# A graph network's dense stage: who adds x to the product, TensorE or VectorE, and over how many PSUM banks

## The reference, cut to what matters

```
def _L0_gnn_ref(Z, U, Dmat, head_w, edge_index):
    ...
    alpha = exp_l / (seg_sum[:, dst] + 1e-16)
    weighted = alpha[..., None] * zs
    agg = jax.vmap(lambda w_: jax.ops.segment_sum(w_, dst, num_segments=N))(weighted)
    w = jax.nn.softmax(head_w)
    ssa = jnp.einsum('k,knr,kdr->nd', w, agg, U)
    Z_half = (1.0 - C) * Z + C * ssa
    DZ = Z_half @ Dmat.T
    residual = Z_half - DZ @ Dmat
    grad_step = Z_half + ETA * (residual @ Dmat)
    return jax.nn.relu(grad_step - ETA * LAM)
...
x = _layernorm(x + _L0_gnn_ref(x, L0_gnn_U, L0_gnn_Dmat, L0_gnn_head_w, edge_index), axis=-1)
x = _layernorm(x + _L1_gnn_ref(x, edge_index, L1_gnn_weight, L1_gnn_attn_l, L1_gnn_attn_r), axis=-1)
```

## Time and profile before

| | us |
|---|---|
| median of 3 runs | 3771.14 |
| lowest and highest run | 3765.44, 3793.86 |
| profiled execution, its own time | 3755.32 |
| its span | 3753.5 |
| dense stage, first to last product | 98.70 |
| last stage behind it | 334.40 |

### The profile page before, as it was taken

The page is one execution under the profiler, slowest core; times in us unless marked ns, Lnnn a source line. Parts: engine busy times, 40 slices in busy tenths (PEclk is TensorE's granted clock), DMA queues, the critical chain, the costliest instruction groups (busy, mean ns, idle before and its releaser), DMA issues. The chain is left out here.

```text
span 3753.5 us, 61674 instructions
## 1 busy us (share of the span) xinstructions
PE 1961.4 (52%) x15249; PEld 1492.6 (40%) x15250; DVE 1919.1 (51%) x5861; ACT 1169.7 (31%) x3041; POOL 1721.7 (46%) x1833
## 2 busy tenths in 40 slices
PE   7344545454555445445445455354444554594776
PEld 7233434333343333333334334243333333453665
DVE  6344545445555445545455455455445544682566
ACT  2012222323323232323223232223232323353557
POOL 3544454444444444444444444544544444224662
PEclk8555555555555555555555555555555555597877
DMA  6211211121221212211112112121211121293343
GB/s 208 52 37 38 48 42 43 39 46 41 48 47 43 44 40 45 47 40 44 42 38 46 42 41 47 41 48 41 47 38 44 40 47 38 65 314 115 120 139 98
DMA packets 406592, 232.96 MB, mean 62 GB/s; under 512 B 284096, under 2 KB 371434, under 8 KB 406506
## 3 DMA queue, kind: packets, MB, share of 16 engines
q1 hardware_dynamic: 346666, 154.11, 15.0%
q0 software_dynamic: 59840, 77.87, 9.7%
HBM read 134.80 MB, written 42.55 MB: 47 GB/s over the span
## 5 line engine op out<-in xcount | busy, mean ns | idle before, releaser
L549 POOL DMA_INDIRECT arena<-z_table,sslot x1563 | 1487.8, 952 | 1702.9 <-SPq L400 1191.5
L1303 PE MATMUL bank<-arena 128*128 x4992 | 609.5, 228 | 564.2 <-issue 474.7
L1538 ACT ACTIVATE arena<-bank 128x272 f32<-128x272 f32 x416 | 268.4, 662 | 1614.6 <-remote 983.0
L1303 PEld LDWEIGHTS bank<-arena 128*128 128x128 bf16 x4992 | 469.3, 107 | 708.9 <-issue 616.4
L850 DVE TENSOR_TENSOR xin<-arena,bank 128x512 f32<-128x512 f32 x208 | 142.9, 687 | 1034.3 <-remote 697.3
L1515 ACT ACTIVATE acc<-xTb 128x68 f32 x1600 | 386.6, 312 | 350.1 <-issue 339.6
L1320 PE MATMUL bank<-xto,arena 128*128 128x68 bf16 x3328 | 330.7, 246 | 218.9 <-issue 218.8
L1320 PE MATMUL bank<-arena 128*128 128x68 bf16 x1664 | 300.3, 244 | 211.1 <-issue 135.0
L1320 PEld LDWEIGHTS bank<-xto,arena 128*128 128x128 bf16 x3328 | 284.7, 132 | 242.1 <-issue 241.7
L1291 PE MATMUL bank<-ident_b,arena 128*128 128x128 bf16 x1664 | 211.0, 306 | 317.9 <-remote 132.1
L841 DVE TENSOR_SCALAR arena<-iota_b,didx 128x128 bf16<-128x128 bf16 x1664 | 302.0, 264 | 40.8 <-issue 34.2
(11 more groups left out here) (250 smaller groups left out, 2493.2 us busy)
## 6 DMA issues: line engine op xcount, KB each, us to landing
arena<-arena SPq DMA_DIRECT2D x1660, 32.0 KB
arena<-z_table,sslot POOLq DMA_INDIRECT x1563
dspace<-in_xT SPq DMA_DIRECT2D x49, 256.0 KB
xmz_table<-agn SPq DMA_DIRECT2D x49, 256.0 KB
x_table<-arena SPq DMA_DIRECT2D x14, 896.0 KB, 4.9
arena<-in_x SPq DMA_DIRECT2D x13, 896.0 KB, 11.0
out<-arena SPq DMA_DIRECT2D x12, 896.0 KB
xin<-in_xT SPq DMA_DIRECT2D x8, 896.0 KB
```

The source lines that it names most:

```text
L549: pool.indirect_dma_start(ring[:, e % RING, :], None, z_table, bass.IndirectOffsetOnAxis(ap=sslot[:, e:e + 1], axis=0)).then_inc(tiles_in[ ...
L1303: last = T.matmul(zd_ps[g % 2][:, u * KR:(u + 1) * KR], onehotT[:, g * G + u, :], z3[:, bass.ds(tiles[u], 1), s, :].rearrange("p a c -> p ...
L1538: A.activation(sums[:, :, 1 + q * Q:1 + (q + 1) * Q].rearrange("p c j -> p j c"), sum_ps[q % 2][:, 0:Q * AW].rearrange("p (j c) -> p j c", ...
```

## The change

`ADDED_BY_PE` becomes (0, 1, 2, 4, 5, 6): TensorE does the second product in six tiles of a group and VectorE its addition in tile 3 alone. The dense stage rotates over six banks (`YD` = 6, banks 2 to 7), so TensorE waits for tile n - 6. The last stage keeps `YB` = 4. One line more at the top shifts all lines behind it by one.

```diff
--- before.py
+++ after.py
@@ -75,8 +75,9 @@
 HALVES = ((0, 4), (4, T7))
 YT = 2
 NY = NT // YT
-ADDED_BY_PE = (0, 2, 4, 6)
+ADDED_BY_PE = (0, 1, 2, 4, 5, 6)
 YB = 4
+YD = 6
 ROOM = NT * D + 64
 GB = 4
 WARM = 64
@@ -1063,7 +1064,7 @@
 
             def add_rows(n):
                 g, t = n // T7, n % T7
-                summed = psum[2 + n % YB][:, 0:D] if t in ADDED_BY_PE else xmz_buf[g % XB][:, t, :]
+                summed = psum[2 + n % YD][:, 0:D] if t in ADDED_BY_PE else xmz_buf[g % XB][:, t, :]
                 return V.scalar_tensor_tensor(row(n), summed, 0.0, row(n), ALU.max, ALU.add)
 
             added = 0
@@ -1076,7 +1077,7 @@
                     dve.wait_ge(y_ps, k + 1)
                     if t not in ADDED_BY_PE:
                         b = xmz_buf[g % XB][:, t, :]
-                        V.tensor_tensor(b, psum[2 + k % YB][:, 0:D], b, ALU.add).then_inc(y_summed, 1)
+                        V.tensor_tensor(b, psum[2 + k % YD][:, 0:D], b, ALU.add).then_inc(y_summed, 1)
                 if 1 <= k <= NT:
                     n = k - 1
                     if n % T7 not in ADDED_BY_PE:
@@ -1415,21 +1416,21 @@
             keep_busy(WARM // 4)
             for n in range(NT):
                 g, t = n // T7, n % T7
-                if n >= YB:
-
-                    if (n - YB) % T7 in ADDED_BY_PE:
-                        pe.wait_ge(y_added, n - YB + 1)
+                if n >= YD:
+
+                    if (n - YD) % T7 in ADDED_BY_PE:
+                        pe.wait_ge(y_added, n - YD + 1)
                     else:
-                        pe.wait_ge(y_summed, summed_by_dve(n - YB))
+                        pe.wait_ge(y_summed, summed_by_dve(n - YD))
                 if t % 4 == 0:
 
                     pe.wait_ge(aT_ready, 2 * g + t // 4 + 1)
                 by_pe = t in ADDED_BY_PE
-                last = T.matmul(psum[2 + n % YB][:, 0:D], aT[g % 2][:, t * P:(t + 1) * P], w3[:, :], start=True, stop=not by_pe)
+                last = T.matmul(psum[2 + n % YD][:, 0:D], aT[g % 2][:, t * P:(t + 1) * P], w3[:, :], start=True, stop=not by_pe)
                 if by_pe:
                     if t == ADDED_BY_PE[0]:
                         pe.wait_ge(xmz_in[g % XB], 16 * (g // XB + 1))
-                    last = T.matmul(psum[2 + n % YB][:, 0:D], ident[:, :], xmz_buf[g % XB][:, t, :], start=False, stop=True)
+                    last = T.matmul(psum[2 + n % YD][:, 0:D], ident[:, :], xmz_buf[g % XB][:, t, :], start=False, stop=True)
                 last.then_inc(y_ps, 1)
                 if t == (1 if g == 0 else 0) and g < NG7 - 1:
                     transpose_sums(g + 1)
```

## The result

Over 20 runs the changed kernel takes 3793.06 us in the median (3779.53 to 3811.42), the kernel before 3769.61 us (3751.31 to 3793.86): ratio 1.0062, with a 95% interval of 1.0044 to 1.0080. It is slower by 17 to 30 us, 23.5 by the medians. The forecast was 21.2 us more and a time of 3792.3. That the time itself came within 0.8 us of the forecast is luck: it was added to a median of 3 runs, 3771.14, which lies 1.5 above that of 20, while single runs of that kernel lie up to 24 us from their median.

The account below looks back on a forecast made before the run. TensorE was taken to set the dense stage's pace. Added products 12.0 us and changes of rows 10.8, less 1.6 at the end, gave 21.2 on the median 3771.14: 3792.3 us, slower by 0.56%, range 3776 to 3810.

Parts of the forecast that it names:

- TensorE sets the pace of the stage: Dense stage: TensorE is never idle, 7.08 us a group, while VectorE is busy 6.73 and lags one tile.
- Prices of 0.43 for a product and 0.20 for a change of rows: TensorE in the dense stage: 0.43 us per tile's product, 0.20 us per change between 64 and 128 rows of weights.
- 28 products and 54 changes, 22.8 us: TensorE in the dense stage: added identity products cost 12.0 us, added changes of rows 10.8 us, together 22.8 us.
- The exception of group 0: First group of the dense stage: transposes stand behind tile 1, so its added changes number 2 instead of 4.
- 1.6 us back at the end: End of the dense stage: last normalisation starts 2.8 us behind the last product instead of 4.43, gaining 1.6 us.
- What VectorE is relieved of: Dense stage: 28 additions of 0.40 us leave VectorE, 11.3 us, its busy time per group falling from 6.73 to about 5.9.
- Adding within 0.1 us of each product: Sign expected in the profile after: VectorE adds each tile of the dense stage within 0.1 us of its product.
- Hidden changes: Rival in the dense stage: changes of rows cost nothing, groups near 7.9 us, time 3781.5 us; chance 0.06.
- VectorE the bound: Rival in the dense stage: VectorE's additions set the pace, so the change saves 10.1 us, time 3761.0; chance 0.05.
- More than 1% slower by something behind the stage: Rival: the shift or TensorE's pause moves the last stage's clock stretches, time from 3809 on; chance 0.09.
- The prediction's own sign of being wrong: Profile after: groups near 7.9 or below 7.08 us, or the rest of the span moving more than a few us.
- about 1%: Whole kernel: the difference that a measurement of it was said to be able to tell from no change.

Follow-up runs that it names:

- banks_only: Changed kernel with TensorE again adding only tiles 0, 2, 4 and 6, six banks kept: dense stage 98.73 us, group 7.08 us.
- six_tiles_four_banks: Changed kernel with four banks in place of six, TensorE still adding in six tiles: dense stage 121.47 us, group 8.72 us.
- padded_four_of_seven: Kernel before the change with w3 and transposed sums zero-padded to 128 rows, four tiles, four banks: dense stage 93.74 us, groups mostly 6.57, one 9.79.
- pairs: Changed kernel with products reordered, two tiles' w3 products then their identity products, 8 changes of rows per group: dense stage 110.50 us, group 7.94 us.
- padded_six: Changed kernel with w3 and transposed sums zero-padded to 128 rows, no changes of rows: dense stage 91.53 us, ratio 0.9984 against the kernel before.
- The padded kernels: Changed kernel zero-padded to 128 rows, without and with rows of x of groups 9 to 13 requested later: ratios 0.9984 and 0.9979 against the kernel before.

## Why the prediction was right

*TensorE sets the pace of the stage.* Right, shown by banks_only and six_tiles_four_banks, and from the other side by padded_four_of_seven, where VectorE's pace of 6.57 came to light only when TensorE's 7.08 was gone. VectorE was closer than a lag of one tile in four suggests: 93% of TensorE's pace.

*Prices of 0.43 for a product and 0.20 for a change of rows.* Right in every kernel in which TensorE is the bound. The stage was to take about 121.5 us and took 121.47; a group 8.74 and 8.72. The attribution to the change of rows was argued from the trace in the prediction, where each identity product brought two changes, so that the two couldn't be told apart by counting; pairs and padded_six show it.

*28 products and 54 changes, 22.8 us.* Measured 22.7 (121.47 - 98.73). The exception of group 0 is 0.4 of that and within what the rows could resolve.

*1.6 us back at the end.* Measured 1.57, with 2.86 us from last product to last normalisation where 2.8 was forecast, but by luck in the path. The forecast added up VectorE's way from the last tile's addition to the root, and put ScalarE's normalisation of group 12 out of the way, ending 2.0 us behind the last product. It ended 2.53 behind it (3438.64 + 3.55 against 3439.66), and the root waited for that. It did so before the change too: the gap between reciprocal and root in the earlier trace rows is 0.25 us and not 0.03, since ScalarE was still normalising until 3406.73. The two ways end within some 0.2 us of each other in both kernels, so the wrong one gave nearly the right sum.

*What VectorE is relieved of.* Mis-sized, without effect on the time: forecast 6.73 to 5.9 us busy for a group, measured 6.30 in a group from the middle of the stage (windows view). The term took 0.40 for each addition that goes, the length of one instruction. But neighbours overlap, the next one starts 0.34 after it while it is recorded for 0.42 (3439.70 in the timeline, its row's statistics at 3440.04; busy time counts an overlap once). That where VectorE waits between tiles this overlap is lost as well is the likely rest of it, not tested. "Adding within 0.1 us of each product" also does not hold for every tile. In the group of the chain above tiles 1, 2 and 6 are added 0.03 or 0.04 us behind their product, tiles 0 and 5 0.13 and 0.11, and tile 4, behind the one addition into the buffer that is left, 0.56. VectorE waited for TensorE ahead of L1068 57 times in 98 tiles.

*The rivals.* Hidden changes: excluded, a group would have been near 7.9. VectorE the bound: excluded. More than 1% slower by something behind the stage: it didn't come, the last stage moved by 0.9 us. The large movements between executions lie ahead of the stage, in the walk over the edges, which the prediction looked for in the wrong place: the stage's first product moved over 46 us between nine executions, while the last stage with its changing clock stayed within a few us. The prediction's own sign of being wrong, that the rest of the span moves by more than a few us, did come in this pair of traces, with the 14.3 us ahead of the stage. No line of the diff acts there. Could the change slow the walk after all? The medians of 20 runs leave 23.5 - 21.2 = 2.3 us for it, and the interval up to 9. The padded kernels, with six banks too, were 5.0 and 9.5 us faster than the kernel before, where their stages give 7.2 and 10.0, with intervals of 8 to 10 us to each side, so nothing points to it. What makes the walk differ between executions wasn't tried. The "about 1%" that a measurement was to tell from no change was too much for 20 runs: their interval is 0.18% to each side.

## What to carry to other kernels

When a pass is moved from one engine to another, first see which of the two sets the pace in that stage: the busier-looking share says little where both are above 90%, but the chain of waits does, and so does the lag of the consumer against the depth of its buffers. On TensorE count not only the products that an edit adds but the runs that it cuts: here nearly half of the loss was the changes between weights of 64 and of 128 rows, and padding the smaller operand with zero rows removed them all while each product took the same 0.43 us. If a stage's length repeats to 0.01 us and whole executions of one kernel differ by tens, judge the edit by the stage.

## What the hardware showed

A change between a product with 64 rows of weights and one with 128 costs 0.196 us in f32 at the full clock, in either direction, within one bank (w3's product to the identity's) or from one bank to another. Between 128*128 and 128*64 it costs nothing: the seven transposes follow the identity product for 0.76 to 0.77 in the chains above, and in padded_six, where w3's product has 128*128, it takes its bare 0.43 right behind them (3349.90). A product of 64 rows and one of 128 take the same 0.43 for 256 columns. Not expected was how exactly these add up. With 0.431 for a product (from padded_six), 0.109 for a transpose (0.76 / 7) and 0.196 for a change (from pairs against after), the sums of the kernels in which TensorE alone is the bound are 98.6 (98.73 measured), 121.3 (121.47), 110.3 (110.50), 132.8 (133.00) and 88.4 (88.75).

The Trainium skill, "TensorEngine Tiling (Array Packing)", section Key Properties, has a drain for every switch of tiling mode. The trace agrees for 64 against 128 rows, at 0.196 us, and disagrees for 128*128 against 128*64, where padded_six shows no time for it in either direction.
